# Three queues around the last block's routing in a fused attention and expert kernel: TensorE takes parts of early tiles 2 and 3 in another order, VectorE takes three steps in another order

## The reference

```python
scores = jax.nn.softmax(xt @ router_w, axis=-1)
expert_weights, expert_idx = jax.lax.top_k(scores, TOP_K)
h = jax.nn.gelu(jnp.einsum('td,edf->tef', xt, w1), approximate=False) * jnp.einsum('td,edf->tef', xt, v1)
y = jnp.einsum('tef,efd->ted', h, w2)
yk = jnp.take_along_axis(y, expert_idx[:, :, None], axis=1)
out = jnp.sum(expert_weights[:, :, None] * yk, axis=1) + bias
```

## Time and profile before

| | us |
|---|---|
| median of 3 runs | 861.97 |
| lowest and highest | 859.67, 863.43 |
| the profiled execution, its own time | 861.95 |
| its span | 860.2 |
| TensorE busy | 817.9 (95%) |
| VectorE busy | 556.8 (65%) |
| ScalarE busy | 376.8 (44%) |
| GpSimd busy | 491.9 (57%) |

### The profile page before, as it was taken

How to read it: one execution, slowest core, us unless ns; L and a number is a source line. 1 busy time by engine, 2 the same in 40 slices (tenths; PEclk the granted TensorE clock), 3 DMA queues, 4 the chain that set the end, 5 groups by cost and what they waited for, 6 DMA issues and landing times.

```text
span 860.2 us, 18943 instructions
## 1 busy us (share of the span) xinstructions
PE 817.9 (95%) x5027; PEld 728.3 (85%) x5028; DVE 556.8 (65%) x1553; ACT 376.8 (44%) x681; POOL 491.9 (57%) x458
## 2 busy tenths in 40 slices
PE   6889999999999989888999999999999999999994
PEld 4668898989888778777999999999999999999993
DVE  6668767778775849766655556555565565555653
ACT  4775656575665515432434334234334342343221
POOL 2363745768695876568743645547437465384333
PEclk9999999999999999979999999999999999999998
DMA  8031050303020271414732422423424222222221
GB/s 283 26 112 50 1 179 1 125 26 100 6 96 15 86 224 36 157 70 121 231 46 46 140 43 37 136 46 96 90 37 135 46 41 43 37 37 39 48 37 18
DMA packets 49421, 67.61 MB, mean 79 GB/s; under 512 B 4896, under 2 KB 43680, under 8 KB 49376
## 3 DMA queue, kind: packets, MB, share of 16 engines
q1 hardware_dynamic: 35712, 47.71, 17.7%
q0 software_dynamic: 13664, 19.35, 12.2%
HBM read 43.51 MB, written 23.54 MB: 78 GB/s over the span
## 4 chain that ended last, share of the span: by engine, by line
PE 85%; POOL 4%; DVE 4%; issue 3%; ACT 2%; DMA 1%; another core or an unknown queue 0%; DVEq 0%; SPq 0%; POOLq 0%; ACTq 0%
PE ps L594 24%; PE ps L595 23%; PE ps L596 23%; PE ps L757 5%; POOL routed L1890 2%; PE ps L723 2%; PE ps L695 1%; PE ps L778 1%; PE ps L777 1%; PE ps L612 1%; PE ps L640 1%; DVE pos_k L1525 1%; PE ps L601 1%; PE ps L682 1%; PE ps L647 1%
## 5 line engine op out<-in xcount | busy, mean ns | idle before, releaser
L594 PE MATMUL ps<-split,xT_moe_hi 128*128 (+2 forms) x426 | 167.2, 392 | 0.2
L596 PE MATMUL ps<-split,xT_moe_hi 128*128 (+2 forms) x426 | 161.1, 378 | 0.0
L595 PE MATMUL ps<-split,xT_moe_lo 128*128 (+2 forms) x426 | 161.1, 378 | 0.0
L1901 POOL TENSOR_TENSOR y_moe<-y_moe 128x256 f32<-128x256 f32 x71 | 67.5, 951 | 129.5 <-DVE y_moe L1569 129.5
L1109 ACT ACTIVATE hidT_hi<-ps 128x768 fp32r<-128x768 f32 x71 | 57.6, 812 | 156.6 <-PE ps L757 156.6
L1910 POOL DMA_INDIRECT out_rows<-y_moe,tok_moe x71 | 111.1, 1565 | 23.3 <-issue 22.7
L594 PE MATMUL ps<-split,hidT_hi 128*128 (+1 forms) x355 | 106.5, 300 | 2.3 <-issue 2.3
L1103 ACT ACTIVATE gelu_moe<-ps 128x704 f32<-128x704 f32 x71 | 53.8, 758 | 123.7 <-PE ps L596 119.3
L595 PE MATMUL ps<-split,hidT_lo 128*128 (+1 forms) x355 | 100.7, 284 | 0.0
L596 PE MATMUL ps<-split,hidT_hi 128*128 (+1 forms) x355 | 100.7, 284 | 0.0
L1569 DVE SCALAR_TENSOR_TENSOR y_moe<-ps,gate_moe,gates 128x256 f32<-128x256 f32 x142 | 62.2, 479 | 56.3 <-PE ps L778 56.1
(11 more groups left out here) (217 smaller groups left out, 2001.1 us busy)
## 6 DMA issues: line engine op xcount, KB each, us to landing
raw<-in_w SPq DMA_DIRECT2D x9, 1408.0 KB
x_moe<-routed SPq DMA_DIRECT2D x74, 132.5 KB
raw<-in_w SPq DMA_DIRECT2D x9, 640.0 KB
x_sb<-in_x SPq DMA_DIRECT2D x8, 512.0 KB, 3.9
x_again<-in_x SPq DMA_DIRECT2D x8, 512.0 KB
out_rows<-x_again SPq DMA_DIRECT2D x8, 512.0 KB
gu_raw<-in_gu_t SPq DMA_DIRECT2D x1, 1536.0 KB, 7.3
raw<-in_w SPq DMA_DIRECT2D x18, 64.0 KB
```

The lines of the kernel that those rows point to most:

```text
L594: pe.matmul(dst, a_hi, b_hi, start=first, stop=False)
L595: pe.matmul(dst, a_lo, b_hi, start=False, stop=False)
L596: return pe.matmul(dst, a_hi, b_lo, start=False, stop=last)
L1901: g.tensor_tensor(y_moe[:, t.slot, 0, :], y_moe[:, t.slot, 0, :], y_moe[:, t.slot, 1, :], ALU.add)\
```

## The change

Nothing is added to or taken from the computation. On TensorE, the last bank of tile 2's first product is now between the two halves of `h2_transposes(7)`; `hid_transposes(Tile(2))` is ahead of `rank_tokens(7)`; and the first two banks of tile 3's first product are between `rank_tokens(7)` and `count_all`. On VectorE, `multiply(Tile(2))` is ahead of `choose(7)`; `count(7)` is ahead of `xT_rest(Tile(3))`; `hidT_rest(Tile(2))` is ahead of `gate_y(Tile(1))`; and `table()` is ahead of `split_lo(v, 0, 2)` (the last third of expert 0's low weights) instead of behind it. The queues of ScalarE, GpSimd and SP are the same.

```diff
@@ TensorE
             first_products(Tile(2), PICKED, AB[:2])
             h2_transposes(7, 0)
+            first_products(Tile(2), PICKED, AB[2:])
             h2_transposes(7, 1)
-            first_products(Tile(2), PICKED, AB[2:])
             router_logits(7)
             x_transposes(Tile(3))
             second_product(Tile(1), PICKED)
+            hid_transposes(Tile(2))
             rank_tokens(7)
+            first_products(Tile(3), PICKED, AB[:2])
             count_all()
-            hid_transposes(Tile(2))
-            first_products(Tile(3), PICKED, AB[:2])
             first_products(Tile(3), PICKED, AB[2:])
@@ VectorE
+            multiply(Tile(2))
             choose(7)
+            count(7)
             xT_rest(Tile(3))
-            count(7)
             take_gates(Tile(2))
             slots(7)
-            multiply(Tile(2))
             weigh(7)
+            hidT_rest(Tile(2))
             gate_y(Tile(1))
+            table()
             split_lo(v, 0, 2)
-            hidT_rest(Tile(2))
-            table()
```

## The result

| | kernel before | changed kernel |
|---|---|---|
| median, lowest and highest (us, 12 runs each) | 861.82, 859.67 to 863.43 | 859.16, 858.10 to 862.64 |
| ratio, 95% interval | | 0.9974 [0.9964, 0.9985] |
| the profiled execution, its span | 861.95, 860.2 | 860.15, 858.4 |

The change gains 2.2 us (1.3 to 3.1 by the interval). The forecast was 858.6, a gain of 3.4. The number is near; the way to it is not the one that the prediction describes, and that is what the rest is about.

A forecast was written before the change was run, and what follows sets the result against it. TensorE was taken as the bound, with its path and tile 5's rows ending almost together. From 861.95 us, 5.1 us for tile 5's earlier start came off and 1.7 us for the clock went on: 858.6, range 856.0 to 862.6.

The forecast's parts named there:

- A: The forecast case: full clock through block 7's scores, ranks read when they end; 858.6 us, range 856.9 to 860.0, chance 0.50.
- the clock then stays up: Block 7's scores: with the extra bank, about 1 us more work, TensorE keeps full clock; scores take 1.95 instead of 3.42 us.
- Ranks read when they end: Block 7's ranks: VectorE reads them as TensorE's last row ends, 372.4 at the latest, without the earlier 2.3 us delay.
- Rival E: Ranks and scatter stay put, VectorE's 2.71 us wait being bound to time, not order; 861.4 us, chance 0.35 together with B.
- I keep both long ones: Block 7's scatter: two transfers beside `split_lo` stay long, 2.50 and 2.22 us against 0.96, so it runs 13.3 us as before.
- 7.3 us earlier: Tile 3's turn on TensorE comes at 383.4 instead of 390.74, but tile 5's rows keep this from being the gain.
- Both paths end almost together: At tile 5 in the kernel before, the rows arrive about 0.6 us ahead of TensorE's own path.
- 1.7 us were charged: Behind an idle TensorE at tile 5: half of a 3.40 us half-clock stretch is added to the time.
- Carried to the end unchanged: From 400 us on TensorE is busy 447.44 of 460.20 us, so any earlier gain or loss reaches the end unchanged.
- C: Slower: tile 2's turn ahead of the ranks delays block 7's routing, `weigh(7)` ending after 378.5; 863.5 us, chance 0.10.
- B: Half clock through block 7's scores, as before; 859.7 to 861.4 us, chance 0.35 together with Rival E.
- D: All 7.3 us of tile 3's turn gets through, needing tile 5's rows by 391.5; 854.6 us, chance 0.05.

The follow-up runs named there:

- dve_only: Changed kernel with TensorE's queue put back to that of the kernel before, VectorE's edits kept: 862.87 us, ratio 1.0002 to the kernel before.
- h2_undone: Changed kernel with tile 2's last bank again behind both halves of `h2_transposes(7)`: 859.98 us, ratio 0.9968 to the kernel before.
- before_pause2: Kernel before, only with GpSimd waiting for block 7's ranks after six of block 6's eight scatter transfers: 860.27 us, ratio 0.9970.
- after_pause2: Changed kernel with GpSimd waiting for block 7's ranks after six of block 6's eight scatter transfers: 857.98 us, ratio 0.9941 to the kernel before.
- rank_first: Changed kernel with `rank_tokens(7)` again ahead of `hid_transposes(Tile(2))` on TensorE: 861.32 us, ratio 0.9984 to the kernel before.
- scatter6_late: Changed kernel with GpSimd waiting for block 7's ranks before it starts block 6's scatter: 867.28 us, one run.
- plain_traffic: scatter6_late plus 24 plain transfers of block 6's rows by SP to an unused place, started while the scores are made: 862.43 us, one run.
- the pauses: GpSimd waits for block 7's ranks after four or six of block 6's transfers, in changed kernel (some with later weights load) or kernel before: ratios 0.9936 to 0.9970.
- the second set: The changed kernel unaltered, timed once more beside the kernel before: 860.21 us against 863.27, ratio 0.9965.

## Why the prediction was right, and where it was not

**The scores.** They ended at +2.9, near the forecast +2.5, at full clock, as A had it. But the reason given was wrong: "the clock then stays up" was ascribed to the extra bank, and dve_only and h2_undone, without it, have the same +2.9. So the half clock in the earlier trace rows did not come from the order of the queue: h2_undone, dve_only and before_pause2 have that order up to the scores and full clock. That the forecast of the scores came out was luck. And "the clock of the stretch from 364.5 on is therefore what matters" was wrong too: before_pause2 had its ranks 4.4 us sooner than the kernel before by that clock, and read them at the same moment as after_pause2.

**`multiply(Tile(2))` ahead of the choice.** Right: the choice starts 1.04 us behind the scores (forecast 1.1), and the ranks are read no later for it.

**The ranks.** This is the step that failed. "Ranks read when they end" put them at +7.8; they were read at +12.2, 3.8 us behind their row. The 2.3 us in the earlier trace rows was treated as a fixed length that might or might not be added; it was the distance to a fixed moment, set by block 6's scatter. Rival E had named the cause as "bound to the time and not to the order", and that is what rank_first, scatter6_late, plain_traffic and the pauses show. E's price was wrong, though: it let only the slack be gained, while the change lets TensorE do tile 2's turn and tile 3's two banks during the wait, and takes the multiplication out from between `slots` and `weigh`.

**The scatter.** Forecast 4.5 us earlier; measured from block 6's mark 1.0, which is the multiplication that no longer stands between `slots` and `weigh`. It ran shorter than charged: of the two long transfers one took 2.50 us and the other 1.22, 376.06 to 388.39 = 12.3 us instead of 13.3. So tile 5's load was issued 2.1 us earlier.

**Which transfers are long.** The Trainium skill, SBUF — State Buffer, section "Who interferes with whom", lets VectorE and GpSimd hold each other up only at their shared port pair, and infers that a VectorE operation on two tensors, which takes only the read side of it, does not hold up the making of descriptors. The rows go against this inference again. A transfer that starts within such a `split_lo` ends 0.82 to 0.85 us after the operation does, wherever it began: 381.73 + 1.76 = 383.49, transfer to 384.32; 384.67 + 1.62 = 386.29, transfer (385.90) to 387.12; in the earlier trace rows 392.22 and 393.04. The transfer at 384.63 began 0.04 us ahead of the operation and took its usual 0.96. So "I keep both long ones" was mis-sized by a margin of 0.04 us; it is 0.05 us in the changed kernel's second profile, with the same lengths.

**TensorE's own path.** "7.3 us earlier" for tile 3's turn became 3.2. The table took 3.9 us as charged (4.0), but could only begin when the ranks were read, 4.4 us later than forecast.

**Tile 5.** No idle time stood there, and the prediction had named this as a sign that it was wrong. Tile 5's rows and marks are 144 packets. The hardware queue had moved them by 392.7, and TensorE came at 394.05, 1.3 us later; in the kernel before they were through by 398.1, 0.8 us ahead of TensorE and not 0.6. "Both paths end almost together" held within about 1 us. The rows moved forward by 2.7 us and TensorE by 2.1, and TensorE's own path sets the gain at tile 5: 2.1 instead of 5.1.

**The clock.** 1.7 us were charged for an idle TensorE at tile 5. The low stretch came earlier: 6.8 us at 0.50 from 383.8 on, against 3.4 in the kernel before, beginning in the 2.72 us wait for tile 3's turn. From that turn on, 5.8 of the 6.8 us are left. They are 2.4 more than before, and half of that, 1.2 us, is an estimate of their cost. Measured, the time from tile 3's turn to tile 5 grew by 1.1 us (9.2 against 8.1), which is part of the 2.1 above and not on top of it. So the charge stood at the wrong place and was 0.6 us too high.

**After 400 us.** "Carried to the end unchanged" was wrong. Tile 5 to tile 9 took 27.4 us instead of 25.9: the output addition of tile 2 now goes out between the base store and expert 2's weights and lands 9.8 us after its issue; in the kernel before it went out 1.2 us ahead of the store, and its 144 packets were through by 406.2, 3.9 us after its issue at 402.26. Tile 6 then waits for its slot. This gave back 1.5 us in one profile of the changed kernel; in the second, 27.5 us, it was the same.

**The sum.** By the trace 0.6 us at tile 30 (0.9 in the second profile) remain of the change. The timed gain is 2.2, and 3.0 in the second set. The traces do not show the timed gain: from block 6's mark to the end of the span the kernel before takes 495.6 us and the changed one 496.6, in its second profile 494.8. The changed kernel's first profile is 1.0 us over its median. That the one profile of the kernel before was a lucky one behind the mark is likely (dve_only, as slow as it by the timing, stands at +203.0 at tile 30 and not at +201.7), but not shown. Against the forecast's 5.1 - 1.7 = 3.4 the trace has 2.1 at tile 5, the clock within it, less 1.5 at tile 6. The timed gain lies between the two, so the number came out nearer than its terms. That is luck, and the range, 856.0 to 862.6, held even the time of no change.

**The rivals.** C's condition was met: `weigh(7)` ended at +14.1, its limit was 378.5 - 364.56 = 13.9. It was not slower, since C left out that the scatter might be shorter and that TensorE's own path is ahead too. B and D did not occur. The chance given to "within 0.5%" covers what came: 0.26%. By the prediction's own chances its range leaves out about 1 in 10 (D, and half of C), not 2.

**What beats both kernels.** The changed kernel with the pause after six transfers: 0.9941 [0.9926, 0.9955].

## What to carry to other kernels

When a wait ends long after its releaser's row, vary the releaser's time before you sum with it: if the reader doesn't move, it is held by something else in flight, and work can be put between at no cost to it, as tile 2's turn was here. Look at what GpSimd has under way at such places; a pause of its indirect transfers ahead of a signal on the path can be worth as much as a new order on the engines that wait (0.9970 against 0.9974). And a step that comes earlier in one queue also meets other transfers: follow it through the next stores, output additions and weight loads before you write that the rest stays as it is.

## What the runs showed of the hardware

Some signals of TensorE's matmuls were seen late by other engines while GpSimd's indirect transfers were under way. With eight transfers the ranks were read 3.8 us (changed), 2.3 us (before) and 5.7 us (rank_first) behind the row; with none of them 0.04 us; with 24 plain transfers of SP 0.03 us. ScalarE is hit as well as VectorE (2.6 us for tile 2's turn in the changed kernel: its row ends at 369.87 and ScalarE starts on it at 372.49; 5.2 us for tile 4's transposes in after_pause2), and so is GpSimd itself (before_pause2). TensorE itself goes on: tile 3's matmuls follow the ranks without a gap.

Not every signal within a scatter is late. In before_pause2 the scores end at +2.93 and the choice starts at +2.97. Within block 7's scatter of the changed kernel, ScalarE starts on tile 4's transposes and on tile 3's turn 0.04 us behind their rows (380.47 to 380.51, 386.35 to 386.39). Nor does every late one wait for the last transfer: after_pause2's tile 4 is read at 383.37, as the seventh of block 7's eight transfers starts (383.34). One of VectorE's signals within block 6's scatter came at once (`xT_rest(Tile(3))` ends at 368.87, tile 2's turn starts at 369.02).

The Trainium skill, Perfetto Trace Analysis, section "Tensor Engine Instruction (MATMUL, LD_WEIGHTS)", says that the shown end of a matmul is an estimate, and that the write's acknowledgement and the signal's way come after it. The rows agree that something lies behind the end, 0.03 to 5.7 us for the ranks. Why the scatter delays it, and what decides which signals are late, stays open.
